# Splitting the cross-attention weights on GpSimd: four pieces in the first slots, or one a period

## What is computed

```python
def cross_attention(x, ctx, wq, wk, wv, wo, bo):      # 20 heads of 64
    q = x @ wq;  k = ctx @ wk;  v = ctx @ wv           # split into heads
    attn = softmax((q k^T) * SCALE)
    return (attn v) @ wo + bo

x = cross_attention(layer_norm(x, g1, be1), layer_norm(x, g1, be1), wq1, wk1, wv1, wo1, bo1) + x
x = cross_attention(layer_norm(x, g2, be2), context, wq2, wk2, wv2, wo2, bo2) + x
```

## Time and profile before

| | |
|---|---|
| median of three runs | 1339.02 us |
| the profiled execution | 1336.38 us, span 1334.6 us |
| mean granted TensorE clock | 0.972 |
| TensorE products busy | 1242.2 us, 93% |
| VectorE busy | 963.4 us, 72% |
| GpSimd busy | 811.6 us, 61% |
| ScalarE busy | 780.4 us, 58% |
| self attention | about 283 to 658 us |

### The profile page before, as it was taken

How to read it: one execution, slowest core, us unless ns; L and a number is a source line. 1 busy time by engine, 2 the same in 40 slices (tenths; PEclk the granted TensorE clock), 3 DMA queues, 4 the chain that set the end, 5 groups by cost and what they waited for, 6 DMA issues and landing times. The chain is left out here.

```text
span 1334.6 us, 38542 instructions
## 1 busy us (share of the span) xinstructions
PE 1242.2 (93%) x16252; PEld 1046.7 (78%) x16252; DVE 963.4 (72%) x1792; ACT 780.4 (58%) x1424; POOL 811.6 (61%) x872
## 2 busy tenths in 40 slices
PE   6988888767999999999889999999999999999698
PEld 4766666656998999899768888888888888887588
DVE  6788888745777777777477867776867777776375
ACT  3577776534665666566365656565656666565265
POOL 2587888638654565456436656565656656577465
PEclk9999999868999999999889999999999999999899
DMA  6111100011000000000010000000010000000000
GB/s 135 24 34 38 51 26 2 1 43 43 2 2 2 2 2 2 2 2 2 2 38 2 8 2 8 3 1 9 1 50 2 2 2 2 2 2 2 14 16 26
DMA packets 31989, 20.34 MB, mean 15 GB/s; under 512 B 21415, under 2 KB 30347, under 8 KB 31819
## 3 DMA queue, kind: packets, MB, share of 16 engines
q1 hardware_dynamic: 31819, 17.88, 5.3%
HBM read 16.56 MB, written 1.31 MB: 13 GB/s over the span
## 5 line engine op out<-in xcount | busy, mean ns | idle before, releaser
L553 POOL TENSOR_TENSOR cross_probs_l<-cross_probs 128x1024 f16<-128x1024 f32 x160 | 302.5, 1893 | 52.2 <-ACT cross_probs L638 52.0
L638 ACT ACTIVATE cross_probs<-cross_score 128x1024 f32<-128x1024 f32 x160 | 164.0, 1025 | 187.1 <-PE cross_score L869 187.0
L723 DVE TENSOR_REDUCE cross_top<-cross_max 128x2 f32<-128x1024 f32 x160 | 195.8, 1223 | 64.0 <-PE cross_max L843 64.0
L1649 POOL TENSOR_TENSOR ad_probs_l<-ad_probs 128x1024 f16<-128x1024 f32 x64 | 120.6, 1893 | 61.2 <-ACT ad_probs L1731 60.8
L553 POOL TENSOR_TENSOR self_probs_l<-self_probs 128x1024 f16<-128x1024 f32 x80 | 151.4, 1892 | 1.2 <-ACT self_probs L638 1.2
L889 PEld LDWEIGHTS cross_pv<-cross_v_h,cross_probs 128*128 128x128 bf16 x1280 | 116.4, 98 | 39.3 <-issue 27.0
L638 ACT ACTIVATE self_probs<-self_score 128x1024 f32<-128x1024 f32 x80 | 81.9, 1024 | 111.2 <-PE self_score L869 111.1
L889 PE MATMUL cross_pv<-cross_v_h,cross_probs 128*128 128x65 bf16 x1280 | 134.5, 195 | 7.1 <-POOL cross_probs_l L553 6.2
L890 PE MATMUL cross_pv<-cross_v_l,cross_probs 128*128 128x64 f16 x1280 | 133.2, 194 | 0.0
L891 PE MATMUL cross_pv<-cross_v_h,cross_probs_l 128*128 128x65 bf16 x1280 | 132.8, 193 | 0.0
L869 PE MATMUL cross_score<-cross_qk_h 64*128 64x256 f32 x640 | 120.4, 373 | 0.0
(11 more groups left out here) (448 smaller groups left out, 4605.9 us busy)
## 6 DMA issues: line engine op xcount, KB each, us to landing
ad_ctx_rows<-in_ctx SPq DMA_DIRECT2D x8, 192.0 KB, 3.0
cw_ctx_rows<-in_ctx SPq DMA_DIRECT2D x8, 192.0 KB, 2.5
sw_raw<-in_L_xattn_wq SPq DMA_DIRECT2D x2, 640.0 KB, 7.0
sw_raw<-in_L_xattn_wk SPq DMA_DIRECT2D x2, 640.0 KB, 4.2
sw_raw<-in_L_xattn_wv SPq DMA_DIRECT2D x2, 640.0 KB, 4.0
cw_raw<-in_L_xattn_wq SPq DMA_DIRECT2D x2, 640.0 KB, 4.7
lr_raw<-in_L_xattn_w_ff SPq DMA_DIRECT2D x2, 640.0 KB
out<-x_rows SPq DMA_DIRECT2D x8, 160.0 KB, 1.9
```

The source lines that it names most:

```text
L553: nc.gpsimd.tensor_tensor(probs_l[:, n % PR, :, :].rearrange("p j k -> p (j k)"), whole, whole.bitcast(BF16)[:, 1::2], ALU.subtract).then_ ...
L638: nc.scalar.activation(probs[:, n % PR, :, :].rearrange("p j k -> p (j k)"), score_bank[:, :], ACT.Exp, scale=SCALE).then_inc(exped, 1)
L723: nc.vector.reduce_max(out, scores, AX.X).then_inc(max_read, 1)
L1649: nc.gpsimd.tensor_tensor(probs_l[:, n % PR, :, :].rearrange("p j k -> p (j k)"), whole, whole.bitcast(BF16)[:, 1::2], ALU.subtract).then_ ...
```

## The change

`split_piece` is taken apart into `high` (the wait for the load and the cast) and `low` (the wait for the cast, the subtraction, the wait for it). GpSimd no longer calls them in the first period. In a steady period whose batch number `cur[0]` is 1 to 4 (the second to fifth period) it does piece `cur[0] - 1`: the cast at the end of slot 5 and the subtraction at the end of slot 8, each after a wait for GpSimd's own low part of the probabilities of that slot.

```diff
-    def split_piece(self, engine, n):
+    def operands(self, n):
         rows = (slice(0, P), slice(0, P), slice(0, CDIM), slice(0, CDIM))[n]
-        low_rows = slice(P // 2, P) if n == 1 else rows
         high = (self.q[0], self.q[2], self.k[0], self.v[0])[n]
         low = (self.q[1], self.q[2], self.k[1], self.v[1])[n]
-        raw = self.raw[n % 2]
-        after(engine, self.split, n)
+        return rows, self.raw[n % 2], high, low
+
+    def high(self, engine, n):
+        rows, raw, high, _ = self.operands(n)
         engine.wait_ge(self.loaded[n % 2], (n // 2 + 1) * 16)
         self.nc.gpsimd.tensor_copy(high[rows, :], raw[rows, :]).then_inc(self.rounded, 1)
+
+    def low(self, engine, n):
+        rows, raw, high, low = self.operands(n)
+        low_rows = slice(P // 2, P) if n == 1 else rows
         engine.wait_ge(self.rounded, n + 1)
         self.nc.gpsimd.tensor_tensor(low[low_rows, :], raw[low_rows, :], high[low_rows, :], ALU.subtract).then_inc(self.split, 1)
         engine.wait_ge(self.split, n + 1)
...
+                if not cross and kind == "steady" and s in (5, 8) and cur[0] <= background.PIECES:
+                    pool.wait_ge(probs_split, cur[0] * RB + (s - SCORE + 1) * ROUNDS)
+                    (background.high if s == 5 else background.low)(pool, cur[0] - 1)
                 if kind == "first":
-                    if not cross and 0 <= s - MAX < background.PIECES:
-                        background.split_piece(pool, s - MAX)
                     if cross and s == 2:
                         split_wo()
```

## The result

The changed kernel takes 1328.09 us, the median of five runs (1322.67 to 1330.2), against 1337.23 for the kernel before (1337.19 to 1340.58): a ratio of 0.9918, with an interval of 0.9895 to 0.994. Measured twice more, with other kernels beside it, the ratio was 0.9934 (0.9918 to 0.995) and 0.994 (0.992 to 0.9959). The mean of the three is 0.9931, a gain of 9.3 us. Each interval is wide beside it: the third alone allows gains of 5.5 to 10.7 us.

What follows compares the result with a forecast made beforehand. TensorE was taken as the bound, held in the first period by GpSimd's queue. Slot sum 9.6 and second reckoning 10.1 us gave 9.7, added work and transfers nothing: 1339.02 - 9.7 = 1329.3 us, range 1326.3 to 1334.3.

Steps and rivals of the forecast that it cites:

- the price of the low clock: First period, two slow TensorE stretches (306 to 314, 323 to 327 us): full clock would give back 4.5 us.
- the second reckoning: First period from totals: 7.0 us of waits and 4.5 of clock go, new waits cost 1.4; gain 10.1 us.
- the clock's rival: First period: clock falls anyway, 4.5 us not given back, gain 5 to 6 us, 1333.5 us; chance 0.15.
- 7.0 us of waits: TensorE's waits for GpSimd, 283 to 325 us: 6.5 us for rounded maxima, 0.5 for the low half; all removed.
- slot by slot sum: First period, queues followed through slots 3 to 7: slot 8 opens at 317.4 instead of 326.66; gain 9.6 us.
- slot 5: First period: scores from 305.5, values from 308.85 to 309.95, weighting to 310.8 us, with two new waits.
- What bounded the first period: First period: GpSimd's order of instructions, not a late input, set TensorE's wait for the maxima.
- the two new waits: Slot 5, first period: TensorE waits 0.5 us on ScalarE's turned copy and 0.9 for the values' transformed rows.
- The strict reading of the rule: First period: clock falls only after an idle window, so no wait of 0.5 or 0.9 us brings it down.
- The rival of another chain: Slots 4 to 7, first period: ScalarE or VectorE holds each by 1.5 us; gain 3 to 4, 1335.6 us; chance 0.09.
- The added work: Periods two to five: cast behind slot 5's low half, subtraction behind slot 8's, hidden under TensorE's work; cost nothing.
- The slower rival: Periods two to five: pieces hold up VectorE's maxima, 4.2 us a period, 16.6 us in all, 1345.9 us; chance 0.05.

Runs made afterwards that it cites:

- e1: Kernel before plus idle TensorE products in front of the turning of the maxima, slots 4 to 7 of the first period; ratio 1.0003 to the kernel before.
- e5: Changed kernel with each piece's cast and subtraction done twice; ratio 0.995 to the kernel before.
- e9: Changed kernel with one piece left in slot 3 of the first period and idle TensorE products in slot 5's two waits; ratio 0.9932 to the kernel before.
- e10: Changed kernel with one piece left in slot 3 of the first period, profiled once more; not timed, slot 9 opened 22.65 us behind the first turning.
- e6: Changed kernel with each piece's cast and subtraction done three times; ratio 1.0066 to the kernel before.
- e4: Changed kernel with one piece left in slot 3 of the first period; ratio 0.9939 to the kernel before.
- e8: Changed kernel with one piece left in slot 3, GpSimd's slot 4 low half held until VectorE finished the transformed rows; ratio 0.9941 to the kernel before.
- e0: The changed kernel run again without alteration; ratio 0.9934 to the kernel before.
- e3: Changed kernel with four raw buffers instead of two, so the transfers load in the first period again; ratio 0.9932 to the kernel before.
- e7: The changed kernel run once more without alteration; ratio 0.994 to the kernel before.

## Why the prediction was right or wrong, term by term

**The step that failed** is the price of the low clock, in the prediction's words that TensorE "pays again for having waited". It stood beside the waits with 4.5 us, in the second reckoning and in the price of the clock's rival, and it drew the sum of 9.6 up to 9.7. The runs showed 0.75 us for the clock (e1) and 9.6 us for GpSimd's queue, where the prediction had 7.0 us of waits less 1.4 of new ones. In the slot by slot sum the mechanism was right, and the term that was mis-sized is slot 5: the values were to begin 8.17 us behind the first turning (308.85 less 300.68) and began 7.62 behind it. That sum came to 9.6 where 10.35 was measured.

**The time.** Forecast 1329.3, a gain of 9.7; measured 1328.09 in the first comparison, a gain of 9.3 us over the three. Faster was right. The range (1326.3 to 1334.3) holds the median but not every run: the fastest of the changed kernel was 1322.67. It allowed too little for the scatter: the first turning alone moves by up to 8 us between executions. That the total came within 0.4 us of the forecast is partly luck, since the intervals are wider than that and the first period by itself gave 10.35.

**What bounded the first period.** Right, and stronger than put. The waits were read as GpSimd's order of instructions; e1 shows that the whole stretch from the first piece to the last was GpSimd's queue.

**Slot by slot.** The blocks of TensorE (1.20, 1.27, 0.83) were right, and so were the places of the two new waits. The first was 0.47 us (forecast 0.5), the second 0.45 (forecast 0.9). ScalarE's timeline of the changed kernel has the two instructions that set them:

```profile
309.10 0.36 ACT L636 CAST self_turned<-self_shared 128x256 bf16<-128x256 f32 x1
...
310.89 0.62 ACT L593 CAST self_ln_h<-self_ln_t 128x512 fp32r<-128x512 f32 x1
```

The turned copy began 4.21 us behind the first turning (forecast 4.36), the cast 1.79 us behind the copy (forecast 2.02, its rows taken from the kernel before), and the values 1.62 us behind the cast (forecast 1.75). Together that is 0.5 us of slot 5. The values themselves took 1.02 us (forecast 1.1) and the slots 6 and 7 3.2 each (forecast 3.3). So slot 8 was forecast 16.7 us behind the first turning and opened 15.93 behind it. That is the difference between 9.6 and 10.35.

**The second reckoning** (waits, plus slow stretches scaled by their clock, 10.1 us) came near the measured sum by luck. It booked 4.5 us to the clock. e1 kept the clock at 1.00 and got 0.75 back. A stretch at a low clock costs only where TensorE is the bound, and between 306 and 325 us GpSimd was. What belongs in its place is the growth of the waits. With the clock held, GpSimd's queue was worth 9.6 us and the new waits took 0.92, so the waits for it come to about 10.5 us, where the list showed 7.0 at the lower clock.

**The rival of the clock.** Its price, 4.5 us, came from the same mistake. Its chance was fair: e5 has the changed kernel's first period, and there the clock was at 0.50 from 303 to 306 us.

```profile
303.00:306.00 3.00, 3.00 (x24) 2.46 (x23) 1.02 (x3) 2.55 (x6) 0.42 (x2) 0.50 0.00 0
```

Slot 9 opened 22.10 us behind the first turning, 0.8 later than where the clock held. So the rival exists, in one of six profiles with that first period, and takes 0.8 us. (In e9 and e10, two of the four runs with a piece in slot 3, the clock fell in slot 4 as well.) The strict reading of the rule in the Trainium skill (TensorE: Matmul & The Clock Gate, part 1), that an idle stretch is what brings it down, did not hold here. Ahead of this fall TensorE had waits of 1.37 and 0.38 us with work between them, and behind the same two waits the clock held in the other five.

**The rival of another chain** did not come: ScalarE and VectorE held TensorE by 0.92 us in slots 4 to 7, not by 6.

**The added work.** Priced at nothing, and it was: 0.15 us of GpSimd's idleness left in slot 5, none in slot 8, TensorE busy 39.89 of 40. The slack of 2.7 us, on which that price rested, measured 2.6 in e5 and e6.

**The slower rival** (the pieces hold up VectorE) was rightly put low for the place where the change puts them: VectorE's maxima take 1.19 to 1.23 us before and after. But e4 and e8 show that its mechanism is real, by another road: a piece need not touch VectorE itself. It can push GpSimd's next instruction onto a VectorE operation with two inputs in SBUF.

## What to carry to other kernels

When a background job sits in an engine's queue ahead of what the bounding engine waits for, look for slots whose idle time and whose users' slack together cover it, and prove the slack by making the job longer. Waits and slow-clock stretches are not to be added up: first ask which engine's queue the stretch follows, since a faster TensorE in another engine's stretch only waits longer. And compare single profiles from a common event behind the stages that scatter.

## What the hardware showed that was not expected

- The clock can fall or hold in the same sequence of instructions: in slot 4 of the first period it was 0.50 in e5 and 1.00 in e0, e3, e6, e7 and the first profile.
- VectorE's subtraction of two SBUF tiles took 0.43 us free, and 0.98, 1.02 and 1.76 us when a GpSimd instruction of 1.9 us had started 1.19, 1.16 and 0.41 us earlier; it ended 0.27 to 0.28 us behind GpSimd. The wait shows as the length of the subtraction and not as idle time in front of it.
- The stretch from the start to the first turning of the maxima in the self attention took between 298.34 and 306.41 us with the same instructions.
